# First vertical sum of three chunks in four moved from VectorE to GpSimd, right neighbour of more chunks on VectorE

## The reference

```python
x = x + conv0(_gn(x), theta_s, w_dw, w_pw)   # layer 0
x = x + conv1(_gn(x), ...)                   # layer 1

def conv0(x, theta_s, w_dw, w_pw):
    # each channel is shifted by its own sub-pixel amount (dy, dx), zero padded:
    s = z1*(1-dy)*(1-dx) + z2*(1-dy)*dx + z3*dy*(1-dx) + z4*dy*dx
    return einsum('bchw,oc->bohw', s * w_dw, w_pw)
```

## Time and profile before

| | |
|---|---|
| median of 3 runs | 5330.59 us (5328.4 to 5332.22) |
| the profiled execution, its own time | 5333.35 us |
| its span, first to last instruction | 5331.7 us |
| outside the span | 1.65 us |
| granted clock of TensorE, mean | 0.963 of full speed |
| first part, to the end of image 7 | some 2650 us, then c1 of image 7 to some 2791 us |

### The profile page before, as it was taken

One profiled execution on the slowest core, in us unless ns is written; L12 is line 12 of the kernel. 1 busy time (PEld: TensorE's weight loads), 2 busy tenths in 40 slices (PEclk: granted clock), 3 DMA queues, 4 the chain that ended last, 5 costly groups with the idle time before them and its releaser, 6 DMA issues. The chain is left out here.

```text
span 5331.7 us, 54963 instructions
## 1 busy us (share of the span) xinstructions
PE 4655.7 (87%) x12634; PEld 2160.9 (41%) x12634; DVE 4621.4 (87%) x4447; ACT 4330.6 (81%) x6469; POOL 1158.6 (22%) x853
## 2 busy tenths in 40 slices
PE   2889999999999999999999999999987777777775
PEld 1334434344343443444434666666642222222222
DVE  8989899998999989999808999999468888888887
ACT  5888888888888888888837888888578888888887
POOL 0000000000000000000006888888211111111111
PEclk7999999999999999999999999999999999999998
DMA  8989999999999999999972333333159999999999
GB/s 344 364 338 374 427 396 422 426 394 427 389 425 426 394 427 392 427 391 346 361 280 96 133 135 132 133 135 135 44 120 225 236 236 236 236 236 236 236 236 223
DMA packets 248867, 1542.06 MB, mean 289 GB/s; under 512 B 29424, under 2 KB 29808, under 8 KB 91504
## 3 DMA queue, kind: packets, MB, share of 16 engines
q1 hardware_dynamic: 156528, 936.14, 44.7%
q0 software_dynamic: 36864, 268.45, 24.3%
q10 hardware_dynamic: 55296, 335.57, 15.2%
HBM read 877.35 MB, written 662.70 MB: 289 GB/s over the span
## 5 line engine op out<-in xcount | busy, mean ns | idle before, releaser
L1175 PE MATMUL ps<-arena,c2T 128*128 128x512 f32 x2048 | 1025.1, 652 | 366.3 <-ACT arena L919 363.7
L997 PE MATMUL ps<-arena 128*128 128x512 f32 x2048 | 968.3, 617 | 19.6 <-DVE small L1340 17.2
L976 PE MATMUL ps<-arena 128*128 128x512 f32 x2048 | 964.9, 598 | 7.7 <-DVE arena L1407 6.5
L972 PE MATMUL ps<-arena 128*128 128x512 f32 x1536 | 743.7, 607 | 105.7 <-ACT ps L625 49.2
L1175 PEld LDWEIGHTS ps<-arena,c2T 128*128 128x128 f32 x2048 | 401.9, 205 | 988.8 <-ACT arena L919 558.7
L919 ACT ACTIVATE arena<-ps,small 128x512 f32<-128x512 f32 x1024 | 713.0, 778 | 98.5 <-DVE arena L1618 90.4
L1502 DVE SCALAR_TENSOR_TENSOR ps<-arena,taps,ps 128x1024 f32<-128x1024 f32 (+1 forms) x602 | 655.5, 1132 | 15.6 <-PE ps L1122 13.7
L625 ACT ACTIVATE ps<-arena 128x1024 f32<-128x1024 f32 x512 | 526.4, 1028 | 161.8 <-ACT arena L666 149.1
L544 POOL TENSOR_SCALAR arena<-arena 128x256 f32<-128x256 f32 x112 | 114.7, 1029 | 2484.6 <-DMA arena<-in_x 2440.1
L666 ACT ACTIVATE arena<-ps,small 128x1024 f32<-128x1024 f32 x512 | 564.3, 1102 | 86.3 <-PE ps L976 85.7
L997 PEld LDWEIGHTS ps<-arena 128*128 128x128 f32 x2048 | 385.9, 189 | 546.1 <-issue 539.9
(11 more groups left out here) (169 smaller groups left out, 6010.4 us busy)
## 6 DMA issues: line engine op xcount, KB each, us to landing
arena<-in_x SPq DMA_DIRECT2D x508, 1024.0 KB, 12.8
out_x<-arena ACTq DMA_DIRECT2D x256, 1024.0 KB, 8.8
out_x<-arena POOLq DMA_DIRECT2D x256, 1024.0 KB, 17.0
arena<-out_x SPq DMA_DIRECT2D x208, 1024.0 KB, 15.0
y_dram<-arena ACTq DMA_DIRECT2D x128, 512.0 KB, 8.3
arena<-y_dram SPq DMA_DIRECT2D x128, 512.0 KB, 3.4
h_dram<-arena SPq DMA_DIRECT2D x112, 512.0 KB, 2.6
arena<-h_dram SPq DMA_DIRECT2D x112, 512.0 KB, 10.2
```

The costliest lines, as they stand in the source:

```text
L972: mm(ps[:, r, :], w_right[:, :], cells(r, 1), start=False, stop=False, skip_group_check=True)
L976: last = mm(ps[:, r, :], w_center[:, :], cells(r, 0), start=False, stop=True, skip_group_check=True)
L997: last = mm(ps[:, 4 + s % 2, :], w_c1b[:, q, :], cells[:, q // 2, q % 2, :, :], start=(q == 0), stop=(q == 3))
L1175: last = mm(ps[:, 4 * k + q, :], c2T[:, q, :], h2[:, k * HC:(k + 1) * HC], start=True, stop=True)
```

## The change

POOL gets a function `add_above`. For chunks 1, 2 and 3 of every group it forms the first vertical sum in two instructions, a `tensor_scalar` (the row above times `up`, to `u`) and a `tensor_tensor` (plus the chunk), each of 2048 elements with its tensors in SBUF. DVE keeps it for chunk 0. DVE waits for POOL before it adds the row below. Image 0 has all its left neighbours on DVE now. Images 1 to 6 have the right neighbour of chunk 3 on DVE, as before; image 7 has those of chunks 1, 2 and 3. Buffers, DMAs and ACT are as they were.

```diff
+POOL_CHUNKS = (1, 2, 3)
+RIGHT_DVE = (SLOTS - 1,)
+RIGHT_DVE_LAST = (1, 2, 3)
...
-        def left_on_pe(b, s):
-            return isinstance(b, int) and b == 0 and s == 1
...
         def three_in_v(b, s):
-            return not (isinstance(b, int) and b == 0) and (s % 2 == 1 if final(b) else s == SLOTS - 1)
+            return not (isinstance(b, int) and b == 0) and s in (RIGHT_DVE_LAST if final(b) else RIGHT_DVE)
...
+            def add_above(b, g, s):
+
+                t = b * NCH + g * SLOTS + s
+                u = u_buf[s][:, :, 1:W + 1]
+                for near in (s - 1, s):
+                    wait_alone(pool, b * (16 * NG) + g * 16 + 16, slot_in[near])
+                wait_alone(pool, nth(t * 2 + 1, 2 * SLOTS), conv_done)
+                pool.tensor_scalar(u, ring[:, s * ROWS:(s + 1) * ROWS, :], up, 0.0, ALU.mult, ALU.add).then_inc(u_above, 1)
+                wait_alone(pool, above_made(b, g, s) - 1, u_above)
+                pool.tensor_tensor(u, u, slot(s), ALU.add).then_inc(u_above, 1)
+
+            def group_rows(b, g):
+                for s in POOL_CHUNKS:
+                    add_above(b, g, s)
+
             def image_rows(b):
+                group_rows(b, 0)
                 copy_bottom(b, 0)
                 with pool.Fori(1, NG - 1) as g:
                     copy_top(b, g)
+                    group_rows(b, g)
                     copy_bottom(b, g)
                 copy_top(b, NG - 1)
-
+                group_rows(b, NG - 1)
...
                 u = u_buf[s][:, :, 1:W + 1]
-                stt(out=u, in0=ring[:, s * ROWS:(s + 1) * ROWS, :], scalar=up, in1=slot(s),
-                    op0=ALU.mult, op1=ALU.add).then_inc(u_up, 1)
+                if s not in POOL_CHUNKS:
+                    stt(out=u, in0=ring[:, s * ROWS:(s + 1) * ROWS, :], scalar=up, in1=slot(s),
+                        op0=ALU.mult, op1=ALU.add).then_inc(u_up, 1)
...
-                dve.wait_ge(u_up, t + 1)
+                if s in POOL_CHUNKS:
+                    dve.wait_ge(u_above, above_made(b, g, s))
+                else:
+                    dve.wait_ge(u_up, b * NG + g + 1)
```

More of the change, by code:

```diff
@@ L130, in preact_kernel @@
         pwT, w_center, w_right = (cut(P) for _ in range(3))
-        w_left = y1_out[0][:, 0:P]
         c1H, w_c1b = (four(cut(4 * P)) for _ in range(2))
@@ L262, in preact_kernel @@
         consts_made = sem("consts_made")
-        setup_done, w_step = sem("setup_done"), sem("w_step")
+        setup_done = sem("setup_done")
         primed = sem("primed")
@@ L278, in preact_kernel @@
         bias0_ready = sem("bias0_ready")
-        u_up, v_done, v_left = sem("u_up"), sem("v_done"), sem("v_left")
+        u_up, u_above, v_done, v_left = sem("u_up"), sem("u_above"), sem("v_done"), sem("v_left")
         top_copied, bottom_copied = sem("top_copied"), sem("bottom_copied")
@@ L325, in first_pairs, with left_made, above_made @@
             return [divmod(n, SLOTS) for n in (2 * s, 2 * s + 1)]
-        def left_on_pe(b, s):
-            return isinstance(b, int) and b == 0 and s == 1
         def v_made(b, g, s):
-            if isinstance(b, int) and b == 0:
-                return g * (SLOTS - 1) + (1 if s == 0 else s)
-            return b * NCH + g * SLOTS + (s + 1 - NG)
+            return b * NCH + g * SLOTS + (s + 1)
         def three_in_v(b, s):
-            return not (isinstance(b, int) and b == 0) and (s % 2 == 1 if final(b) else s == SLOTS - 1)
+            return not (isinstance(b, int) and b == 0) and s in (RIGHT_DVE_LAST if final(b) else RIGHT_DVE)
+        def left_made(b, g, s):
+            k = len(RIGHT_DVE)
+            if final(b):
+                return g * len(RIGHT_DVE_LAST) + ((B - 2) * NG * k + RIGHT_DVE_LAST.index(s) + 1)
+            return b * (NG * k) + g * k + (RIGHT_DVE.index(s) + 1 - NG * k)
+        def above_made(b, g, s):
+            k = 2 * len(POOL_CHUNKS)
+            return b * (NG * k) + g * k + (2 * POOL_CHUNKS.index(s) + 2)
         def final(b):
@@ L563, in image_rows @@
                     copy_top(b, g)
+                    group_rows(b, g)
                     copy_bottom(b, g)
                 copy_top(b, NG - 1)
+                group_rows(b, NG - 1)
+            pool.wait_ge(setup_done, 1)
             image_rows(0)
@@ L958, in conv @@
                 k = s % 2
-                near = 1 if left_on_pe(b, s) else 0
                 def cells(r, dx):
-                    return u_buf[s][:, 2 * r:2 * r + 2, near + dx:near + dx + W]
+                    return u_buf[s][:, 2 * r:2 * r + 2, dx:dx + W]
                 for half in range(2):
                     if half == 0:
[L966 to L969, removed]
+                        pe.wait_ge(v_done, v_made(b, g, s))
                     pe.wait_ge(x_in_psum, nth(t * 2 + half))
@@ L972, in conv @@
                         mm(ps[:, r, :], w_right[:, :], cells(r, 1), start=False, stop=False, skip_group_check=True)
-                    for r in range(2 * half, 2 * half + 2) if left_on_pe(b, s) else ():
-                        mm(ps[:, r, :], w_left, cells(r, -1), start=False, stop=False, skip_group_check=True)
                     for r in range(2 * half, 2 * half + 2):
@@ L1396, in shift_rows @@
                     count_x(*ahead_of, s, range(2, DVE_PIECES))
[L1397 to L1410, removed]
+                dve.wait_ge(u_done, nth(t))
+                v, beside = u_buf[s][:, :, 0:W + 1], u_buf[s][:, :, 1:W + 2]
+                left_added = stt(out=v, in0=v, scalar=left, in1=beside, op0=ALU.mult, op1=ALU.add)
+                if three_in_v(b, s):
+                    left_added.then_inc(v_left, 1)
+                    if ahead_of and not late:
+                        count_x(*ahead_of, s, range(2, DVE_PIECES))
+                    dve.wait_ge(v_left, left_made(b, g, s))
+                    v = u_buf[s][:, :, 0:W]
+                    stt(out=v, in0=u_buf[s][:, :, 1:W + 1], scalar=right, in1=v,
+                        op0=ALU.mult, op1=ALU.add).then_inc(v_done, 1)
+                else:
+                    left_added.then_inc(v_done, 1)
                 if late and not final(b):
@@ L1437, in _ @@
             x_scales(1)
-            ts(tmp, scale0, left, None, ALU.mult).then_inc(w_step, 1)
-            dve.wait_ge(w_step, 1)
-            ts(w_left, pwT[:, :], tmp, None, ALU.mult)
             dve.wait_ge(late_in, 16 * len(LATE_PARAMS))
```

## The result

| | before | after |
|---|---|---|
| median | 5329.49 us (4 runs, 5325.93 to 5332.22) | 5683.14 us (4 runs, 5677.35 to 5684.22) |
| ratio | | 1.0662, 95% interval 1.0643 to 1.0680 |
| span of the profiled execution | 5331.7 us | 5682.5 us |

The kernel became 354 us slower. The forecast was 5805, the range 5600 to 5990.

A forecast was written before the change was run, and what follows sets the result against it. ACT's order was taken as the bound, DMA close behind; with POOL and DVE taking turns, DVE becomes it. Image 0 +81.9, images 1 to 6 +295.8, image 7 +93.7 on 5333.35 give 5805 us, range 5600 to 5990.

The forecast's parts named there:

- row copies and one-element instructions: Evidence for turns: a POOL row copy took 2.61 us behind a DVE sum, a one-element DVE instruction 2.37 beside POOL.
- The small delay of the earlier trace: A DVE sum just behind a POOL row copy took 2.48 us in place of 2.33, the least loss considered, 0.15.
- checks named in advance: Signs expected in the profile after, such as DVE sums averaging some 4 us and image 0 taking some 379 us.
- POOL's lengths: POOL's two instructions of 2048 elements, put at 2.07 us (`tensor_scalar`) and 4.56 us (`tensor_tensor`) from shorter ones.
- POOL's turns: Time POOL takes from DVE in each first-part group: 19.05 us plus two row copies at 0.27, 19.6 us.
- The statistics pieces: DVE's 7.1 us of `bn_stats` a group in images 0 to 6: half hidden under POOL, 3.5 us kept.
- The same starts and ends of images: Time beyond the eight groups of an image stays 28.7 us (image 0), 9.4 (images 1 to 6), -1.0 (image 7).
- with DMA close behind: In the first part before the change, ACT's order sets the pace, 33.6, 39.9 and 35.4 us a group, DMA next.
- the four squares of the earlier trace: Timeline of ACT's squares in image 2, giving 9.985 us a chunk, 39.9 us for a group of four.
- The win: Rival: POOL's instructions hardly hold up DVE's sums in the first part, ACT's pace holds, 5294 us; chance 0.07.
- All pieces hidden: Rival: POOL always finds its turn under statistics pieces, all 7.1 us a group hidden, 5609 us; chance 0.10.
- Late loads: Rival: POOL needs slots some 6 us before DVE, so one 2.8 us load wait a group, 5962 us; chance 0.10.

The follow-up runs named there:

- run 1: The kernel before, with POOL in image 0 also running the two instructions for chunks 1 to 3 into an unused block, DVE not waiting: 5414.91 us, ratio 1.0154.
- run 3: The changed kernel with no chunk on POOL: DVE makes all first sums and keeps the neighbours it got in images 0 and 7: 5332.28 us, ratio 1.0001.
- run 8: The changed kernel with all first sums of the first group of every image on DVE: 5608.15 us, ratio 1.0517 to the kernel before.
- Run 7: The kernel before, with ACT's two passes over its quarter of the chunk ahead cut from 512 to 8 elements: 5319.86 us, ratio 0.9979.

## Why the prediction was right, and where its sizes were off

**The direction and the mechanism** held at each link. That POOL and a sum take turns for their whole lengths was read from row copies and one-element instructions; it holds for instructions of 2048 elements (DVE's sum of 5.67 us above) and with nobody waiting (run 1). The small delay of the earlier trace rows was no guide to long instructions. Most checks named in advance came out: sums well over 2.34 us, `bn_stats` at 0.68, `tensor_tensor` near 6 us behind a sum, PE waiting for L1424, later parts unchanged. Some did not, as the loss was smaller: the DMA share is 0.92 in images 1 to 6, not below 0.9, and ACT waits for PE 4.5 us a group (217.1 in 48 groups), not 5 to 12. The sums were expected at 4 us on average; they are at 3.2 (the 647 records of L1390, L1412, L1424 and L1431), with part of POOL's turn falling on column copies (1.11 us in place of 0.17).

**The total** was 122 us too high, a third of the measured loss. By stretches:

| | forecast | measured |
|---|---|---|
| image 0 | +81.9 | +40.5 |
| images 1 to 6 | +295.8 | +225.9 |
| image 7 | +93.7 | +86.8 |

*POOL's lengths.* The step "2.14 ns an element more: 4.56" took the slope between 896 and 1024 elements, and this small difference of two means was too steep: alone the `tensor_tensor` takes 4.16, the `tensor_scalar` 1.96 for 2.07. POOL's turns are thus 3 x (1.96 + 4.16 - 0.28) + 0.5 = 18.0 us a group and not 19.6. That is 1.6 us in each of 64 groups, some 100 us. In images 1 to 6 the two errors below nearly cancel each other, so the 70 us there are about POOL's lengths; that they cancel is luck.

*The statistics pieces.* With 18.0, a group of images 1 to 6 has 22.7 + 0.3 + 18.0 = 41.0 us that exclude each other and takes 43.0: 2.0 of 7.1 stay visible, not 3.5. In image 0 it is 42.0 - 38.7 = 3.3. In image 7, which has no pieces, the sum is 45.5 against 45.0 measured. That it comes so close is partly luck: run 3 shows that without pieces between them sums cost 2.37 us each there ((35.8 - 0.3) / 15), and with that the sum would be 46.7.

*"The same starts and ends of images"* failed twice, in opposite directions. In images 1 to 6 what is beyond eight inner groups was taken as 9.4 us and is 366.5 - 8 x 43.0 = 22.5. Most of it is the first group, 55.9 us in image 3. DVE is idle in it for 2.4 us (before 1200.66, waiting for PE). Some 4.5 us are the short instructions at an image's start, by which the first group was longer before, too (41.5 for 37.0 in image 2). The rest, some 6 us, is that more of POOL's turns fall on DVE: four `tensor_tensor` instructions in place of three, the last of them on the copy at 1225.00. Which part of this comes of the late weights is open (run 8). In image 0, the first and last group (43.5 and 47.7 us, again from first sum to first sum) are about as long as before (44.2 and 47.2), though POOL works in them. So 337.7 - 8 x 42.0 = 1.7 us are left over there and not 28.7.

**What bounds the kernel before** was put down to ACT, "with DMA close behind". Run 7 shows that ACT did not bind images 1 to 6. A low wait of ACT for PE did not prove that ACT sets the pace; ACT's chunk took 9.985 us with the DMAs full, and a view of waits can't say which would stay when the other goes. Nor was the pace an even 39.9: in image 2 the groups took 41.5, 37.0, 37.2, 39.7, 41.7, 43.0, 44.7 and 44.8 us, and the four squares of the earlier trace rows come from the middle. The six inner groups of images 1 to 6 average 40.6, which would leave some 4 us for the ends of an image and not 9.4.

**The rivals.** The win needed less than 1.6 us of delay for each POOL instruction. DVE's instructions in the stretch of image 3 that is shown lost 3.3 us to one `tensor_tensor`. "All pieces hidden" (5609) is nearer to the total than the forecast (74 us off against 122), but not for its reason: 2.0 us a group stay visible in images 1 to 6 and 3.3 in image 0, between none and the forecast's half. Late loads did not show as a cost: DVE's wait for loads is gone from the waits. POOL waits for them instead, 482.9 us in 99 waits in images 1 to 6, but it is ahead of DVE, and DVE idles only 0.6 us before L1412.

## What to carry to other kernels

Before work moves from VectorE to GpSimd, look for what each of them does while the other runs: here, a sum with both tensors in SBUF and a POOL instruction that reads SBUF did not overlap at all, while `bn_stats` did, and moving a sum of 2.3 us cost 5.85 us of DVE's time in turns. A short instruction that is mysteriously long in the trace of before, once explained, was worth more than all busy shares. And an engine's spare time has to be checked against the transfers: images 1 to 6, at a DMA share of 0.99, gave nothing back when ACT's work was cut (run 7).

Not tried: a form in which POOL needs one instruction for the sum in place of two, a fix for the late weights that keeps POOL in the first group, which would show what they cost, and any change to the DMAs, which is where run 7 points. No version here beats the kernel before with the computation complete.

## What the runs showed of the hardware that I had not expected

- A memset of 2048 elements on POOL leaves a DVE sum at 2.34 us but stretches a copy of eight cells from 0.17 to 1.61 us; the sum behind it is not late for it, as it starts while the copy's record still runs (240.59 in 240.52 to 242.13). Four of the 28 copies of image 0 took 1.3 to 1.7 us in that run. Beside POOL's reading instructions the copy was 4.18 us once (1351.55), and the sum behind it started only with its end (1355.64).
- The `tensor_tensor` of POOL took 2.37 us at 1024 elements and 4.16 at 2048, so 1.75 ns an element from one size to the other, where 896 to 1024 gave 2.14.
- One input does not make a DVE instruction safe beside POOL. `bn_stats` stays at 0.68 us, but the `tensor_scalar` of 256 elements at an image's start (L1288) goes from 0.35 to 4.26 us at 434.84, and that of 512 elements (L1357) from 0.48 to 2.20 at 1222.82.
